# Delta stage: the triangular inverse in 64x64 quadrants, with each power kept beside its transpose

## The reference, cut to what matters

```
T   = (I - C)^-1            # C: 128x128, strictly triangular, masked K K^T times decays
Z   = T (V - decay * K S)   # corrected values of the chunk
Y   = decay * Q S + (masked Q K^T * decays) Z
S  <- decay * S + K^T (u * Z)
out += silu(gate) * rmsnorm(Y) @ W_out
```

## Time and profile before

| what | us |
|---|---|
| median of 3 runs | 6041.69 (6040.69 to 6044.21) |
| span of the profiled execution, first to last instruction | 6046.2 |
| PE busy in that span | 5221.5 |
| DVE busy | 3480.2 |
| ACT busy | 3055.8 |
| POOL busy | 1178.3 |
| first to last `collect` (L1179), 64 stages between them | 283.9 to 3394.5 |

### The profile page before, as it was taken

The page is one execution under the profiler, slowest core; times in us unless marked ns, Lnnn a source line. Parts: engine busy times, 40 slices in busy tenths (PEclk is TensorE's granted clock), DMA queues, the critical chain, the costliest instruction groups (busy, mean ns, idle before and its releaser), DMA issues. The chain is left out here.

```text
span 6046.2 us, 91895 instructions
## 1 busy us (share of the span) xinstructions
PE 5221.5 (86%) x32318; PEld 3893.8 (64%) x32318; DVE 3480.2 (58%) x6531; ACT 3055.8 (51%) x8923; POOL 1178.3 (19%) x1352
## 2 busy tenths in 40 slices
PE   5799999999989999989999699899998597399969
PEld 4477777877877778877887555555555354255545
DVE  3466666676666667666766566555552554543331
ACT  2466666666656666666666344344441244325421
POOL 0222222322222222222232100011110321002210
PEclk7799999999999999999999799899999798688879
DMA  2000000000000000000000100100000100000000
GB/s 85 19 19 17 13 19 19 18 17 17 19 19 13 17 19 19 17 14 19 22 19 13 46 1 1 65 1 0 0 0 20 27 1 13 21 1 1 1 21 14
DMA packets 51094, 103.57 MB, mean 17 GB/s; under 512 B 12848, under 2 KB 20176, under 8 KB 49520
## 3 DMA queue, kind: packets, MB, share of 16 engines
q1 hardware_dynamic: 50672, 98.07, 5.4%
HBM read 90.43 MB, written 5.52 MB: 16 GB/s over the span
## 5 line engine op out<-in xcount | busy, mean ns | idle before, releaser
L896 ACT ACTIVATE dh_pb<-bank 64x128 f32<-64x128 f32 x3072 | 831.4, 271 | 272.5 <-PE bank L670 239.3
L684 PE MATMUL bank<-dh_cw,dh_pb 128*128 128x128 f32 x5120 | 701.5, 281 | 113.0 <-ACT dh_pb L896 111.4
L684 PEld LDWEIGHTS bank<-dh_cw,dh_pb 128*128 128x128 f32 x5120 | 635.5, 193 | 191.1 <-ACT dh_pb L896 164.4
L1034 DVE SCALAR_TENSOR_TENSOR dh_kq<-bank,dh_conv_kq,dh_kq 128x511 f32<-128x511 f32 (+2 forms) x408 | 305.4, 749 | 184.8 <-ACT dh_kq L853 173.6
L902 ACT ACTIVATE dh_cw<-bank 128x256 f32<-128x256 f32 x640 | 244.9, 385 | 255.1 <-PE bank L684 247.9
L621 PE MATMUL bank<-hT,dh_w_kq 128*128 128x512 f32 x544 | 276.7, 633 | 83.2 <-DVE dh_kq L1034 75.3
L1034 DVE SCALAR_TENSOR_TENSOR dh_v<-bank,dh_conv_v,dh_v 128x511 f32<-128x511 f32 (+2 forms) x384 | 284.2, 747 | 91.3 <-ACT dh_v L853 82.2
L1797 PE MATMUL bank<-moe_h_split,moe_w 128*128 128x512 bf16 x1200 | 277.1, 381 | 14.6 <-PEq L89 14.6
L633 PE MATMUL bank<-dh_w_vz,hT 128*128 128x256 f32 x1024 | 245.5, 383 | 22.0 <-ACT dh_zs L864 22.0
L1128 DVE TENSOR_TENSOR dh_zz<-dh_zz,bank 128x512 f32<-128x512 f32 x130 | 89.2, 686 | 283.0 <-PE bank L597 281.1
L621 PE MATMUL bank<-hT,dh_w_vz 128*128 128x512 f32 x512 | 242.5, 596 | 8.6 <-DVE dh_v L1034 8.6
(11 more groups left out here) (416 smaller groups left out, 12170.8 us busy)
## 6 DMA issues: line engine op xcount, KB each, us to landing
dh_rates<-delta_rates SPq DMA_DIRECT2D x130, 256.0 KB, 3.6
dh_w_vz<-in_L_wvz SPq DMA_DIRECT2D x17, 512.0 KB, 3.3
mod_w<-in_L_wmod SPq DMA_DIRECT2D x4, 1536.0 KB, 7.0
dh_w_kq<-in_L_wkq SPq DMA_DIRECT2D x18, 256.0 KB, 2.6
dh_wo<-in_L_wo SPq DMA_DIRECT2D x16, 256.0 KB, 4.2
moe_w<-in_L_w13T SPq DMA_DIRECT2D x1, 3200.0 KB, 15.7
later_gates<-mod_gate SPq DMA_DIRECT2D x3, 1024.0 KB, 4.0
gate<-later_gates SPq DMA_DIRECT2D x6, 512.0 KB, 3.4
```

Source lines behind the costliest of these rows:

```text
L684: last = pe.matmul(square(j)[:, b, :, :], pb[j][:, b, :], src[:, :, b, :], start=True, stop=True)
L896: last = act.activation(out[half, :, o, half], src[halves[o], :, half], ACT.Copy)
L1034: dve.scalar_tensor_tensor(y, pj_bank(n)[:, 0:S - i], taps(n)[:, TAPS - 1 - i:TAPS - i], y, ALU.mult, ALU.add).then_inc(s["v_cs" if i < TA ...
```

## The change

What it does, part by part:

- `start_power` writes the whole 128x128 C of each sequence (tile `c`, 128x512) instead of two pairs of half tiles. `turn_c` and `c_copy` transpose it once per stage (tile `ct`), four full transposes for a head.
- `first_level` and `level` compute three things for each diagonal 64x64 block: the next power, its transpose (as the product of the transposes, so that no level transposes again) and the next partial product of the inverse. Each product is 64x64x64; it reads one half of the partitions and writes one half, so it uses one of four quadrants of the array; two PSUM banks take the two row halves. Both heads use the same two banks in turn, so level (i, 1) waits for the copy of level (i, 0) and so on.
- `level_copy` (ACT, two copies of 128x384, or 128x256 at level 4) brings all three back. `plus` (POOL) forms I + power^T, which the third product of the next level waits for.
- Level 5 forms the last partial product and, in four products more for a head, its transpose. `last_copy` (ACT, six copies of 64x128) places the diagonal blocks in `ttb`; `cross` and `corner` (8 products each) and their copies `cross_copy` and `corner_copy` make the off-diagonal block. `ttb` then holds the full inverse.
- `w_prod`, `x_prod`, `w_copy`, `zeta`, `off_diagonal`, `turn_power`, `power`, `power_c`, `grow` and `inverse` go. `z_copy` is followed directly by `pu` and `update`.
- The lists are written anew: one slot of side work between one half-level and the next. `decay` moves ahead of `normed` on DVE, and `qk_mask` stays behind `start_power`; `gated_out` moves behind four of the `plus` on POOL. The transposes' bank moves from 0 to 2. `squares` waits for `w_out` of an earlier stage instead of `x_prod`.

```diff
+    ids = sb("ids", [P, HALF])
+    ttb = sb("ttb", [P, RPH, NB, P])
+    lv = sb("lv", [P, RPH, 2, 2, 3, HALF])
...
-    TURN, SQUARE, PJ_A, PJ_B, B_REC, B_AUX = 0, (1, 2), 3, 4, (5, 6), 7
+    LEVEL, TURN, PJ_A, PJ_B, B_REC, B_AUX = (0, 1), 2, 3, 4, (5, 6), 7
...
+    def first_level(pe, t, j):
+        h = hs[j]
+        pe.wait_ge(h["a_ct"], t + 1)
+        if j == 0:
+            after(pe, s["a_y"], t)
...
+            pe.wait_ge(hs[0]["a_lv"], 5 * t + 1)
+        for kind in (POW, TPOW, INV):
+            for sl in range(2):
+                for more in range(2 if kind == INV else 1):
+                    for g in range(2):
+                        for o in range(2):
+                            c = ci[j][halves[g], 2 * sl + o, halves[g]]
+                            cT = ct[j][halves[g], 2 * sl + o, halves[g]]
+                            one = ids[halves[g], :]
+                            lhs, rhs = ((cT, c), (c, cT), (one if more else cT, one))[kind]
+                            last = pe.matmul(lvl[g][halves[g ^ o], sl, kind, :], lhs, rhs, start=(more == 0),
+                                             stop=(kind != INV or more == 1), skip_group_check=True)
+        last.then_inc(h["t_lv"], 1)
...
+    def level(pe, t, i, j):
+        h = hs[j]
+        pe.wait_ge(h["a_lv"], 5 * t + i)
...
+        for kind in (POW, TPOW, INV):
+            if kind == INV:
+                pe.wait_ge(h["p_qi"], 5 * t + i)
+            if i == 4 and kind == POW or i == 5 and kind != INV:
+                continue
+            for sl in range(2):
+                for g in range(2):
+                    for o in range(2):
+                        w = lv[halves[g], j, g ^ o, sl, :, :]
+                        lhs = (w[:, TPOW, :], w[:, POW, :], qi[j][halves[g], g ^ o, sl, :])[kind]
+                        last = pe.matmul(lvl[g][halves[g ^ o], sl, kind, :], lhs, w[:, kind, :], start=True, stop=True)
...
+    def cross(pe, t):
+        for j in HEADS: pe.wait_ge(hs[j]["a_x"], t + 1)
...
+    def corner(pe, t):
+        pe.wait_ge(s["a_g"], t + 1)
...
     def z_prod(pe, t, j):
...
-        after(pe, h["v_ttb"], t)
+        after(pe, s["a_y"], t)
...
     def pu(pe, t, j):
...
-        pe.wait_ge(h["v_x"], t + 1)
+        pe.wait_ge(h["a_zs"], t + 1)
...
+        turn_c(pe, t, 0)
+        v_turn(pe, t, 0)
+        if old:
+            for j in HEADS: ks(pe, t, j)
+        turn_c(pe, t, 1)
+        v_turn(pe, t, 1)
+        side_tensor(pe, q, a, 0)
+        z_prod(pe, t, 0)
+        first_level(pe, t, 0)
+        z_prod(pe, t, 1)
+        if old: qs(pe, t, 0)
+        first_level(pe, t, 1)
+        side_tensor(pe, q, a, 1)
+        pu(pe, t, 0)
+        level(pe, t, 1, 0)
+        if old: qs(pe, t, 1)
+        side_tensor(pe, q, a, 2)
+        level(pe, t, 1, 1)
+        pu(pe, t, 1)
+        side_tensor(pe, q, a, 3)
+        level(pe, t, 2, 0)
+        if a: ku(pe, t, 0)
+        side_tensor(pe, q, a, 4)
+        level(pe, t, 2, 1)
+        if a: ku(pe, t, 1)
+        side_tensor(pe, q, a, 5)
+        level(pe, t, 3, 0)
+        side_tensor(pe, q, a, 6)
+        kk_prod(pe, t)
+        level(pe, t, 3, 1)
+        side_tensor(pe, q, a, 7)
+        side_tensor(pe, q, a, 8)
+        level(pe, t, 4, 0)
+        qk_prod(pe, t)
+        level(pe, t, 4, 1)
+        side_tensor(pe, q, a, 9)
+        for j in HEADS: y_turn(pe, t, j)
+        level(pe, t, 5, 0)
+        w_out(pe, t, 0)
+        level(pe, t, 5, 1)
+        w_out(pe, t, 1)
+        cross(pe, t)
+        corner(pe, t)
...
+    def level_copy(act, t, i, j):
+        act.wait_ge(hs[j]["t_lv"], 6 * t + i + 1)
+        kinds = slice(TPOW if i == 4 else POW, INV + 1)
+        for r in range(2):
+            last = act.activation(lv[:, j, r, :, kinds, :], lvl[r][:, :, kinds, :], ACT.Copy)
+        last.then_inc(hs[j]["a_lv"], 1)
...
+    def plus(pool, t, i, j):
+        h = hs[j]
+        pool.wait_ge(h["a_lv"], 5 * t + i)
+        pool.tensor_tensor(qi[j][:, :, :, :].rearrange("p r s n -> p (r s) n"),
+                           lv[:, j, :, :, :, :].rearrange("p r s k n -> p (r s) k n")[:, :, TPOW, :], mask_bc(ids[:, :], NB),
+                           ALU.add).then_inc(h["p_qi"], 1)
...
+        dve.tensor_tensor(ci[j][:, :, :], kkm[:, :, :], et[j][:, :, :], ALU.mult).then_inc(h["v_u"], 1)
```

More of the change, by code:

```diff
@@ L675, in square_power @@
-    def square_power(pe, t, i, j):
-        h = hs[j]
-        pe.wait_ge(h["a_pb"], 6 * t + i + 1)
-        if i:
-            pe.wait_ge(h["v_c"], 5 * t + i)
-        else:
-            after(pe, h["v_ttb"], t)
[L682 to L685, removed]
+        pe.wait_ge(h["a_ct"], t + 1)
+        if j == 0:
+            after(pe, s["a_y"], t)
+        else:
+            pe.wait_ge(hs[0]["a_lv"], 5 * t + 1)
@@ L707, in z_prod @@
             pe.wait_ge(h["a_vs"], t + 1)
-        after(pe, h["v_ttb"], t)
+        after(pe, s["a_y"], t)
         src = x0[j] if c else vs[j]
[L710 to L721, removed]
+        each(pe, B_REC[j], lambda b: ttb[:, j, b, :], lambda b: src[:, b, :]).then_inc(h["t_z"], 1)
     def qs(pe, t, j):
@@ L1027, in convolve @@
+        side_silu(act, q, a, 6)
+        level_copy(act, t, 4, 1)
+        side_scalar(act, q, a, 9)
+        for j in HEADS: y_copy(act, t, j)
+        last_copy(act, t, 0)
+        side_silu(act, q, a, 7)
+        last_copy(act, t, 1)
+        cross_copy(act, t)
+        corner_copy(act, t)
     def convolve(dve, q, n):
@@ L1238, in vector_stage @@
+        side_vector(dve, q, a, 7)
+        if a == 2: key_vectors(dve, q)
+        if a == 3: query_vectors(dve, q)
         for j in HEADS: normed(dve, t, j)
-        for j in HEADS: grow(dve, t, 5, j)
+        for j in HEADS: start_power(dve, t, j)
         qk_mask(dve, t)
-        for j in HEADS: decay(dve, t, j)
-        for j in HEADS: start_power(dve, t, j)
-        inverse(dve, t, 0)
         collect(dve, t)
-        inverse(dve, t, 1)
     def next_gates(pool, q, kh):
@@ L1470, in _ @@
             for j in HEADS: v_turn(pe, 0, j)
-            for f in (ks, z_prod, w_prod, x_prod, qs, pu, y_turn):
+            for f in (ks, z_prod, qs, pu, y_turn):
                 for j in HEADS: f(pe, 0, j)
@@ L1481, in _ @@
         def _(dve):
-            for f in (rhs, zeta, q_state, output, normed):
+            for f in (rhs, q_state, output, normed):
                 for j in HEADS: f(dve, 0, j)
```

434 lines of the change are left out of this document (151 added, 283 removed).

## The result

The changed kernel takes 5859.7 us (median of 4 runs, 5853.3 to 5882.8) against 6043.0 for the one before, measured beside it on the same chip. The ratio is 0.970, with a 95% interval of 0.968 to 0.972. That is faster by 183 us, inside the range, and 145 us above the 5715 forecast: the change gave a little over half of what was worked out for it.

The account below looks back on a forecast made before the run. TensorE's own work was taken as the bound, 42.7 of 48.6 us a stage. Removing 16.8 and adding 11.7 gains 5.1 a stage, so 6041.7 - 64 x 5.1 = 5715 us; 8-in-10 range 5530 to 6150.

Parts of the forecast that it names:

- PE's work: TensorE, per stage: 16.8 us removed, 11.7 added (0.9 transposes, 8.5 small products, 2.3 form changes), a gain of 5.1.
- price of a record: Small 64-wide products on TensorE: 0.014 us a record, from 0.056 for a round of four; 560 records a stage.
- change of form: TensorE switching between full array and tiles: 0.09 us each, 26 changes in 13 blocks, 2.3 us a stage.
- Waits shrink too: Rival: TensorE's waits per stage fall from 5.9 to 3 us, giving 5530; chance 0.15 for below 5630.
- feeding rival: Rival: small-product records can't be fed that fast; at 0.027 us each, 6140 us; chance 0.20.
- two-quadrant version: Variant of slow feeding: only rows or only columns overlap, 280 rounds of 0.056 = 15.7 us, 6175; within the 0.20.
- I leave the 5.9 of before in place: TensorE's waits, handoff tails and loop turns per stage: kept at 5.9 us, though new waits were counted as 3 to 5.
- 1.3 late: DVE's tail with a = 3: `qk_mask` ends 7.4 us after `kk_prod`, PE reaches `w_out` after 6.1, so 1.3 us wait.
- about 2 late: DVE's tail with a = 0: a convolution of 2.2 us stands in it, so `y_turn` is about 2 us late.
- walk: Step through a stage's handoffs in order, looking for waits not covered by PE's work: 3 to 5 us found.
- handoff rival: Rival: DVE's tail, POOL's order or slower bursts add 2 to 3 us waits a stage, 5875; 0.15 for 5830 to 6029.
- two of the signs named for it: TensorE waits longer than 1 us on `plus` (POOL) or on `qk_mask` would show handoffs eating part of the gain.

Follow-up runs that it names:

- experiment 2: The changed kernel with DVE's tail reordered to `kk_mask`, `normed`, `decay`, `qk_mask`, side work, `start_power`: 5700.7 us, ratio 0.944 to the kernel before.
- experiment 4: The changed kernel with the small products of levels 1 to 3 issued twice, 288 records more a stage: 6098.4 us, ratio 1.010 to the kernel before.
- experiment 7: The kernel before with only DVE's tail reordered as in the change, `decay` ahead of `normed` and `qk_mask` behind `start_power`: 6208.1 us, ratio 1.027.
- experiment 6: The changed kernel with loops turned so two small-product calls in a row use the same quadrant, levels 1 to 5: 5893.7 us, ratio 0.976 to the kernel before.

## Why the prediction was right, and what it mis-sized

- **PE's work.** The prediction took 16.8 us off a stage and put 11.7 on. The price of a record stands (15 ns against 14). The change of form was sized too low: a pair costs 0.35 us and not 0.18, which with 1 ns more a record makes a block some 0.2 us longer, and 13 blocks a stage up to 2.7 (an estimate). PE's own gain is then nearer 2.5 us than 5.1; by busy time it is 4.0, from 44.4 to 40.4 in experiment 2 at the same clock of 0.99. No run tells the two figures apart.
- **Luck has a part.** With the tail put right the stage is 43.5 us, just the forecast, and the whole gain 338 to 340 us against 327. But in that kernel the idle time also fell, from 4.2 us a stage before to 3.1. So it is the sum that came true: less saved in work, and some of the old waits gone, which the prediction had only as a rival ("Waits shrink too").
- **The feeding rival** fell by experiment 4, and its two-quadrant version with it: a round of two would have made the block 1.3 us. The Trainium skill ("TensorE: Matmul & The Clock Gate", section "Back-to-back issue gap") has about 25 ns as the least from start to start for up to 64 columns. The trace does not agree for quadrant work: 48 records have 15 ns from start to start, and 48 more in a block cost 14.6 each.
- **The step that was mis-sized** is "I leave the 5.9 of before in place". The same paragraph had seen both new waits, "1.3 late" for `qk_mask` and "about 2 late" for `y_turn`. It then set them against the old 5.9 as if they were part of it. By the prediction's own count the changed stage of 45.8 us holds 45.8 - 37.6 = 8.2 of waits and handoffs, 2.3 more than were left in place, and 64 x 2.3 = 147 is about the miss of 145. (The dearer changes of form and the clock are in that 8.2.) The largest of the old waits were those of the removed level chain (74 of some 168 us from 1000 to 3000 us), and the new ones belong to another edit of the same diff, the moved `decay` and `qk_mask`, which experiment 7 prices at 166 us. As a term of its own it would have given 5715 + 166 = 5881, 21 us above the measured time.
- **What the tail cost was also sized too low.** The walk used 0.69 and 0.7 us for `normed` and `start_power`, which take 0.94 and 1.02 on the mean of all stages; `qk_mask` was late in three kinds of stage (33 waits in 44 stages), and the longest, 2.3, stand at a = 2, not at the a = 3 that was named; and the clock, 0.97 instead of 0.99, adds most of the 60 us by which the same records keep PE busy longer than in experiment 2.
- **The handoff rival** (5830 to 6029, worked out at 5875) is what the measured time and two of the signs named for it point to: `qk_mask` waited for over 1 us, and `plus` for 1.1 at level 4 with a = 3. The first carries it; the second is 11.6 us in 44 stages.
- **The walk's other waits held:** `corner` on `cross_copy` 0.5 idle where 0.7 was forecast, `level` (4, 0) with a = 3 1.1 against 1.2.
- **DVE** saved 5.8 us a stage instead of 8.5. Of the missing 2.7 some 1.6 are the same slowing: `normed` 932 ns instead of 695 and `start_power` 1029 instead of the 690 reckoned, two of each a stage; the gating of the output 994 instead of 763 and `update` 841 instead of 692, one and a half of each. GpSimd has ten `plus` a stage beside them. The rest was not found.

Experiment 2 gave back most of the 60 us of clock. How much of its 0.99 is left to gain was not tried.

## What to carry to other kernels

When a diff swaps a computation and also reorders an engine's queue, price the two apart: run the old kernel with the new order. In this case that one kernel would have shown +166 us beside a gain of about 340. In a queue that several others wait on, put first what the bounding engine waits for soonest, and ask what each instruction releases on a third engine when it moves.

## What the hardware showed unasked

**VectorE beside GpSimd.** Grouping the 128x512 instructions of the changed kernel (1000 to 3000 us) by whether a long GpSimd instruction lies beside them (under 20 ns of it, or over 300) gives these means:

```
VectorE instruction, where its sources lie     alone     beside GpSimd
normed and start_power, both SBUF             0.68 us    1.03, 1.14 us
update, gating of the output, both SBUF       0.69       0.99, 1.07
masks, q_state, output: one in PSUM           0.69       0.68 to 0.69
norms, one source in SBUF                     0.68       0.68
```

(`normed` has none alone in this kernel; 0.68 is `start_power`'s.) Of these instructions only those with two full sources in SBUF are slowed, by 0.3 to 0.45 us. Two cases do not fit so simple a rule. `decay`, a scan with both sources in SBUF, takes 1.20 us beside GpSimd and 1.21 alone in this kernel, but 1.50 beside it in experiment 2. And one 128x16 instruction with a single source (L1071) takes 0.63 us here and 0.16 in experiment 2. GpSimd pays too: `plus` takes 0.72 us alone and 1.47 beside `decay`, in the stage shown above.

```profile
2294.70 1.47 POOL L1223 TENSOR_TENSOR dh_qi<-dh_lv,dh_ids 128x256 f32<-128x256 f32 x1 [1.60 <-ACT dh_lv L929]
2296.41 0.72 POOL L1223 TENSOR_TENSOR dh_qi<-dh_lv,dh_ids 128x256 f32<-128x256 f32 x1 [0.24 <-ACT dh_lv L929]
```

The Trainium skill ("SBUF — State Buffer", section "SBUF: two separate sides") says that a VectorE instruction with two SBUF inputs and a GpSimd instruction that reads SBUF exclude each other on one pair of ports. The trace agrees on which of the 128x512 instructions suffer; that one waits for the whole of the other it doesn't show, since the records overlap and stretch by less than the partner's length.

**Quadrants.** Four 64x64 products share the array with starts 15 ns apart, and almost without regard to the order of the calls (experiment 6). Going from full-array work to them and back costs 0.35 us for the pair: 1.06 less 0.71. It shows in three places: 0.10 in the full-array work ahead, 0.15 between the last small product and the next full one, and 0.10 in the full-array work behind.

**The clock answers to single waits.** Stages with the same records ran at 1.00 or 0.96, and of the stages looked at only those with a single wait of over 2 us dipped, though not each of them. In experiment 2, with these waits gone, they stand at 1.00, but for a stage at the turn of the loop (0.93), where PE stands still for some 6 us.
